# Where a recurrence step's product and state lie: PSUM bank and two states, or SBUF and four states

## The reference, cut to what matters

```python
def step(M, inp):
    q_t, k_t, v_t, g_t = inp
    M = M * decay + jnp.einsum('bhr,bhd->bhrd', g_t * k_t * scale, v_t)
    y = jnp.einsum('bhr,bhrd->bhd', q_t, M)
    return (M, y)
...
_, Y = jax.lax.scan(step, M0, xs)
```

## Time and profile before

| what | us |
|---|---|
| median of three executions | 2109.43 |
| lowest and highest of the three | 2106.26 and 2111.22 |
| the profiled execution's own time | 2107.98 |
| its span, from the first to the last instruction | 2106.2 |
| what lies around the span | 1.8 |

### The profile page before, as it was taken

How to read it: one execution, slowest core, us unless ns; L and a number is a source line. 1 busy time by engine, 2 the same in 40 slices (tenths; PEclk the granted TensorE clock), 3 DMA queues, 4 the chain that set the end, 5 groups by cost and what they waited for, 6 DMA issues and landing times.

```text
span 2106.2 us, 47667 instructions
## 1 busy us (share of the span) xinstructions
PE 2012.6 (96%) x19694; PEld 1489.6 (71%) x19694; DVE 1551.4 (74%) x2004; ACT 1235.6 (59%) x1590; POOL 1439.4 (68%) x686
## 2 busy tenths in 40 slices
PE   6899999999999999999999999999999997779998
PEld 5677777777777777777777777777777743335466
DVE  6677777877777778777777787777777736887757
ACT  4576767666767676666666766666666662111333
POOL 3677777777777777777777777777777756633227
PEclk8999999999999999999999999999999998889999
DMA  5401010301010103010101030101010110212222
GB/s 144 108 20 26 17 28 20 87 16 28 15 29 14 33 21 83 14 29 14 29 14 39 20 78 14 29 14 29 14 29 4 50 36 1 76 35 91 76 61 71
DMA packets 46180, 81.95 MB, mean 39 GB/s; under 512 B 7152, under 2 KB 29168, under 8 KB 45584
## 3 DMA queue, kind: packets, MB, share of 16 engines
q1 hardware_dynamic: 45968, 78.90, 13.6%
HBM read 73.83 MB, written 5.05 MB: 37 GB/s over the span
## 4 chain that ended last, share of the span: by engine, by line
PE 79%; DVE 12%; issue 4%; POOL 2%; ACT 1%; SPq 1%; DMA 0%; POOLq 0%; DVEq 0%; ACTq 0%
PE ps L507 19%; PE ps L499 16%; PE ps L473 12%; PE ps L462 10%; PE ps L491 7%; PE ps L670 6%; DVE amx L1298 4%; DVE Otn L1320 2%; DVE V L1283 1%; PE ps L522 1%; PE ps L453 1%; PE ps L650 1%; POOL qm L1758 1%; PE ps L557 1%; DVE KL L1279 1%
## 5 line engine op out<-in xcount | busy, mean ns | idle before, releaser
L1821 POOL TENSOR_TENSOR acc<-acc,PR 128x1024 f32<-128x1024 f32 x480 | 1150.9, 2398 | 347.2 <-ACT PR L1167 308.0
L1298 DVE TENSOR_REDUCE amx<-ps 128x2 f32<-128x1024 f32 x512 | 623.4, 1219 | 190.4 <-PE ps L491 184.9
L1167 ACT ACTIVATE PR<-ps 128x1024 f32<-128x1024 f32 x512 | 518.8, 1019 | 207.8 <-PE ps L499 194.0
L507 PE MATMUL ps<-PR,V 128*64 128x256 f32 x4096 | 499.4, 386 | 0.4 <-ACT PR L1167 0.3
L507 PEld LDWEIGHTS ps<-PR,V 128*64 128x64 f32 x4096 | 271.1, 136 | 164.3 <-issue 27.1
L1021 ACT ACTIVATE ps<-NM 128x1024 f32<-128x1024 f32 x231 | 236.6, 1026 | 203.2 <-DVE V L1283 176.5
L473 PE MATMUL ps<-wv,C 64*128 64x256 f32 x4608 | 316.2, 281 | 1.2
L499 PE MATMUL ps<-qh,KH 64*128 64x256 f32 x2048 | 310.6, 297 | 6.2 <-ACT ps L1021 6.0
L473 PEld LDWEIGHTS ps<-wv,C 64*128 64x128 f32 x4608 | 306.0, 187 | 11.9 <-issue 4.3
L462 PE MATMUL ps<-C,wk 64*128 64x512 f32 x2304 | 306.4, 393 | 2.6 <-DVE wk L1550 1.5
L499 PE MATMUL ps<-ql,KH 64*128 64x256 f32 x2048 | 293.0, 280 | 0.0
(11 more groups left out here) (199 smaller groups left out, 1906.8 us busy)
## 6 DMA issues: line engine op xcount, KB each, us to landing
wk<-wk_split SPq DMA_DIRECT2D x60, 192.0 KB, 3.2
wv<-wv_split SPq DMA_DIRECT2D x30, 384.0 KB, 4.8
bc<-wm_rows SPq DMA_DIRECT2D x32, 256.0 KB, 4.2
we<-in_we SPq DMA_DIRECT2D x10, 768.0 KB, 4.3
craw<-in_ctx SPq DMA_DIRECT2D x28, 256.0 KB, 4.1
wq<-in_wq SPq DMA_DIRECT2D x32, 128.0 KB, 2.9
wo<-in_wo SPq DMA_DIRECT2D x64, 64.0 KB, 2.2
craw<-in_ctx SPq DMA_DIRECT2D x28, 128.0 KB, 4.1
```

The costliest lines, as they stand in the source:

```text
L507: mm = pe.matmul(psO[half(h), :], V[:, c * KT + 2 * hf + k, hd * DH:hd * DH + DH], PR[:, slot, h, k, :], start=(first and hf == 0 and k == ...
L1167: act.activation(PR[:, pr_slot(t, hf), :, :, :].rearrange("p h k n -> p (h k n)"), ps[:, bank:bank + 2, :].rearrange("p h n -> p (h n)"), ...
L1298: dve.tensor_reduce(amx[:, :, t, c], first_max(n) if pair == 0 else psG, AX.X, ALU.max).then_inc(g_max, 1)
L1821: pool.tensor_tensor(flat(acc[:, :, :, :]), flat(acc[:, :, :, :]), flat(PR[:, pr_slot(t, hf), :, :, :]), ALU.add).then_inc(acc_done, 1)
```

## The change

The product of a step is written to SBUF, into the place of the state, and the scan reads it there and writes over it. There are four states, in two tiles `M` and `M2` of two states each, where there were two. PE's wait for a bank is for the product (`kv_ready`) and no longer for the scan (`m_done`). DVE's wait for POOL is for step J - 4 where it was for step J - 2, and stands ahead of the product where it stood ahead of the scan. POOL reads the state from its new place. The new tile stands behind `gb`, so that the norm's small tiles of the recurrence move by 4 KB.

```diff
+        state_of = lambda J: (M2 if J % 4 >= 2 else M)[:, J % 2, :]
...
                 if J >= 2:
-                    pe.wait_ge(m_done, J - 1)
+                    pe.wait_ge(kv_ready, J - 1)
...
                 dve.wait_ge(vb_ps, J + 1)
-
-                bank = ps[:, 4 + J % 2, :]
-                dve.tensor_tensor(bank, bank, kk[:, g, :], ALU.mult).then_inc(kv_ready, 1)
+                if J >= 4:
+                    dve.wait_ge(qm_ready, J - 3)
+                state = state_of(J)
+                dve.tensor_tensor(state, ps[:, 4 + J % 2, :], kk[:, g, :], ALU.mult).then_inc(kv_ready, 1)
                 dve.wait_ge(kv_ready, J + 1)
-                if J >= 2:
-                    dve.wait_ge(qm_ready, J - 1)
-                dve.tensor_tensor_scan(M[:, J % 2, :], dect[:, g, :], bank, 0.0, ALU.mult, ALU.add).then_inc(m_done, 1)
+                dve.tensor_tensor_scan(state, dect[:, g, :], state, 0.0, ALU.mult, ALU.add).then_inc(m_done, 1)
...
-                pool.tensor_tensor(qm[:, J % 8, :], M[:, J % 2, :], qr[:, n % 2, :], ALU.mult).then_inc(qm_ready, 1)
+                pool.tensor_tensor(qm[:, J % 8, :], state_of(J), qr[:, n % 2, :], ALU.mult).then_inc(qm_ready, 1)
```

More of the change, by code:

```diff
@@ L54, in program @@
         norm_tiles = lambda x: [("st6" + x, [P, NR, 6], F32), ("mv" + x, [P, NR, 2], F32), ("rs" + x, [P, NR], F32)]
-        (w4, bd, rope, t1, t2, gate, uT, dect, qr, kk, vh, vl, M, qm, selvr, ow, vecs, u, seq, sely, dl, dec, gb, *st_a) = room(
+        (w4, bd, rope, t1, t2, gate, uT, dect, qr, kk, vh, vl, M, qm, selvr, ow, vecs, u, seq, sely, dl, dec, gb, M2, *st_a) = room(
             ("w4", [P, 4, 2, DM], F32), ("bd", [P, 2, 2, 2, P], F32), ("rope", [P, 2, W], F32), ("t1", [P, 2, W], F32),
@@ L60, in program @@
             ("ow", [P, 2, DM], F32), ("vecs", [P, 3, DM], F32), ("u", [P, NR, DM], F32), ("seq", [P, W], F32),
-            ("sely", [P, 4, 32], F32), ("dl", [P, 2], F32), ("dec", [P, 2], F32), ("gb", [P, 2], F32), *norm_tiles("a"))
+            ("sely", [P, 4, 32], F32), ("dl", [P, 2], F32), ("dec", [P, 2], F32), ("gb", [P, 2], F32), ("M2", [P, 2, W], F32), *norm_tiles("a"))
         yT = uT
+        state_of = lambda J: (M2 if J % 4 >= 2 else M)[:, J % 2, :]
         selv = qm[:, 0:4, :].rearrange("p a n -> p (a n)").rearrange("p (e c) -> p e c", e=16)
```

## The result

The changed kernel takes 2125.5 us in the median of four executions (2121.71 to 2127.52), the kernel before 2109.0 beside it: a ratio of 1.0075, with a 95% interval from 1.0058 to 1.0092. It is slower by 16.5 us (by the interval, 12 to 19); 2126 was forecast. The profiled execution is the lowest of the four: 2121.71 us, its span 2119.9, so 13.7 us above the profiled execution of before. What follows on single stages is read from the profiled executions; whole kernels are compared by their medians.

What follows compares the result with a forecast made beforehand. Five stages with different limits: POOL in A, PE in B and E, no full engine in C, mostly DVE in D. Terms +9.3, +6.7 and +0.7 make +16.7 us, against the median 2126 us, range 2112 to 2136.

Steps and rivals of the forecast that it cites:

- Held scans: Scans with two SBUF inputs and POOL's instructions exclude one another; a held scan ends 1.08 us behind POOL's end.
- Stage A: 1749 to 1782 us, beside the attention's end: twelve scans hold POOL, +11.6, -3.2 and +0.9 us, together +9.3.
- Stage B: Up to 1804 us: PE at granted clock 0.54 sets steps some 3 us apart, so 0 us change.
- Stage C: To 1845.6 us, steps 20 to 35: scan, bias and POOL's product take turns, 2.95 us a step, +6.7 us.
- Stages D and E: D, to 1900 us: one pair of steps costs +0.7 us; E, with PE always busy: 0, under DVE's spare time.
- The waits: DVE's product waits for PE up to 1900 us, 12.8 us before the change, should nearly be gone.
- Rival 1: Scan and POOL do not hold each other, so waits go: 2101.5 us, at best 2095; chance 0.09.
- Rival 2: They exclude each other and PE also falls to the lower clock in C and D: 2133 us; chance 0.10.
- Rivals 3 and 4: Rival 3: only stage C pays, 2117 us, chance 0.06; rival 4: losses come back, within 4 us of 2109, 0.05.

Runs made afterwards that it cites:

- e7: Against before: four states, the change for steps 16 to 31 alone, their decay tile copied to PSUM so one scan input is there; 2102.52 us, ratio 0.9968.
- e8: Against before: four states, the change for steps 16 to 31 alone, both scan inputs in SBUF; 2110.12 us, ratio 1.0011.
- e2: Kernel before with four states in place of two, the product left in PSUM; 2105.81 us, ratio 0.9987.
- e1: Kernel before with product and scan in SBUF alone, two states and all of PE's waits as before; 2126.75 us, ratio 1.0087.
- e6: Against before: four states, product left in PSUM, PE's products rotating over three banks from step 16 to 33; 2101.71 us, ratio 0.9969.
- e5: Changed kernel without POOL's sixteen bias additions between steps 20 and 35; 2119.62 us, ratio to before 1.0055.
- e3: Against before: the change for steps 0 to 13 only, later products in PSUM, four states throughout; 2116.09 us, ratio 1.0039.

## Why the prediction was right

The forecast was 2126.0 us and the median is 2125.5. Point by point, in the profiled executions (+16.7 forecast there, +13.7 measured), and from one step's product to another's:

**Held scans.** The end of a held scan was put at 1.08 us behind POOL's end, from other instructions; 1.08 and 1.09 were measured. The longest scan is 2.89 us, not over 3. That one rule, taken over from two other pairs of instructions to the scan, carried the forecast, and e7 against e8 shows it to be the cause.

**Stage A.** +9.3 forecast up to step 16; steps 0 to 16 take 9.4 us more. Two errors within it cancel, which is luck. The fold ends 38.53 us after step 0 where it was 28.01: +10.5, not 11.6. Every scan from step 2 to step 12 holds one POOL instruction, but for 0.8 to 0.9 us and not for 0.97: `acc` takes 3.25 to 3.29 us for 2.37, `qm` 2.18 to 2.20 for 1.27, the fold 2.06 for 1.27. Step 1's scan, itself held by POOL's first product, makes POOL start its second one 0.65 us later. These make 10.5 together. One gap was not foreseen: at step 10 DVE waits 3.28 us for PE, whose product stands behind attention products that wait 5.23 us for ACT's `PR`, and POOL's second-last `acc` runs undisturbed in 2.37 us. POOL had work all the time, so the fold is not later for it:

```profile
1777.20 2.37 POOL L1821 TENSOR_TENSOR acc<-acc,PR 128x1024 f32<-128x1024 f32 x1
...
1778.23 0.69 DVE L1405 TENSOR_TENSOR M<-ps,kk 128x512 f32<-128x512 f32 x1 [3.28 <-PE ps L604]
```

So `copy_l` comes 39.75 us after step 0 where it was 32.32: +7.4 for a forecast of 8.4. The 3.2 us that four states were to bring back there are borne out: e2, with the states alone, is 3.05 us shorter up to `copy_l` than before, and e1, with two states and PE's old wait, takes 43.53, 3.8 more than the changed kernel. From `copy_l` to step 16 it is 10.76 us where it was 8.77: +2.0 for a forecast of 0.9. That term left out that the last `divide` would be held as well (1.42 us, the last rows below), which is 1.0 of it.

**Stage B.** 0 forecast, -1.1 measured. PE does set the pace there towards the end: DVE waits for it ahead of steps 18 to 20. Its granted clock came out at 0.64 and not 0.54, which the forecast held fixed: from step 16 to 20 the same 27 matmuls keep PE busy for 7.94 us where it was 9.07, which is the 1.1. e2, whose scans are not held, has 12.23 us there too, and e6 13.81, so the scan is not what shortens it.

**Stage C.** +6.7 forecast, +5.5 measured. The turn was put at 2.95 us and is 2.83: the bias takes 0.52 us behind a scan, not 0.60, and POOL's product 1.23 from its start to the next instruction's, not 1.27. e5, without the bias, has the turn at 2.43.

**Stages D and E.** +0.7 and 0 forecast, +0.3 and -0.2 measured (E to the end of the span).

The sum is 13.9 us against 16.7: C was put 1.2 us too high, B 1.1, D 0.4 and E 0.2, and A 0.1 too low. That the medians came out half a microsecond from the forecast is in part luck: the profiled execution is the lowest of its four, and the interval of 12 to 19 us holds the one sum as well as the other.

**The waits.** DVE's waits for PE were to be nearly gone; 7.8 of 12.8 us are left, 3.3 of them in the gap at step 10.

**The rivals.** Rival 1, a scan that is not held, falls with the first `acc`. Rival 2, the lower clock in C and D, falls with 0.93 and 0.88 in the rows, against 0.92 and 0.87 before. Rivals 3 and 4, that only C pays or that all comes back, fall with stage A and e3. What rival 1 said of the kernel without the hold was too little on one term: 1.5 us for step 12's scan, where e2 gained 3.05 us at `copy_l`. Its sum, 2101.5 us, can be set beside e6 and e7, which leave the scans undisturbed and reach 2101.71 and 2102.52; their edits differ from the change, so that it is the size that agrees, not the sum's terms.

## What to carry to other kernels

Before a DVE operand moves from PSUM to SBUF, count how many of the instruction's inputs then lie in SBUF, and look at what POOL does at that time: with a second SBUF input the two took turns in every run here, even for a scan. Turns don't show as waits; they show as a spread in the durations of a line that had none, and as busy time that grows with no work added. If it is an earlier bank or state that is wanted, a third bank (e6), or the other operand in PSUM (e7), brought some 7 us together with the four states, where the move to SBUF cost 16.5.

## What was not expected of the hardware

The scan from SBUF alone is as fast as from PSUM (1223 to 1224 ns at the shortest, against 1221), so the price lies only in what POOL does beside it. One line that was not touched was hit as well: the last `divide`, whose inputs are in SBUF in both kernels, took 1.42 us at 1791.77 beside POOL's products, where its line has 415 ns at the shortest and 421 in the median:

```profile
1788.27 6.06 POOL L1758 TENSOR_TENSOR qm<-M,qr 128x512 f32<-128x512 f32 x4
```

```profile
1791.77 1.42 DVE L1327 TENSOR_TENSOR Otn<-Ou,Otn 128x256 f32<-128x256 f32 x1
```

POOL was late, so its four products ran on in a row to 1794.33 and reached into DVE's way. And the granted clock of PE moved through edits that leave PE's matmuls of the stage as they were: from 0.54 to 0.64 in B, and in C the same four matmuls took 3.18 us in before and 1.88 in e2. Some 1 us went with it in either place, as much as a term of the sum. What decides it was not tried.
